# Degree inverses of a graph network: made per block inside a pipeline, or for all blocks ahead of it

## What is computed

```
x = layernorm(x + segment_sum(w * x[src], dst) @ W0.T)        # layer 0
x = layernorm(x + L1(x))   # two GCN convolutions with batch norm, then a dense layer
x = layernorm(x + L2(x))   # weighted sum over edges, two-layer MLP
x = layernorm(x + L3(x))   # one GCN convolution with layer norm
# a GCN convolution:
deg  = segment_sum(1, dst) + 1        # with self loops
dinv = 1 / sqrt(deg)
out[d] = sum over edges of (x @ W)[s] * dinv[s] * dinv[d]
```

## Time and profile before

| | before |
|---|---|
| time, median of 3 runs | 3458.49 us |
| profiled execution: time | 3460.09 us |
| profiled execution: span of its trace | 3458.8 us |
| outside the span | 1.3 us |
| block pipeline: first load issued, last load issued | 1270.4, 1375.2 us |

### The profile page before, as it was taken

How to read it: one execution, slowest core, us unless ns; L and a number is a source line. 1 busy time by engine, 2 the same in 40 slices (tenths; PEclk the granted TensorE clock), 3 DMA queues, 4 the chain that set the end, 5 groups by cost and what they waited for, 6 DMA issues and landing times. The chain is left out here.

```text
span 3458.8 us, 60258 instructions
## 1 busy us (share of the span) xinstructions
PE 2842.7 (82%) x19203; PEld 2100.9 (61%) x19220; DVE 1983.2 (57%) x6763; ACT 1275.6 (37%) x3485; POOL 2462.4 (71%) x2238
## 2 busy tenths in 40 slices
PE   5989877878888859789977997778888875699995
PEld 4777655656666648444446774366666764466664
DVE  7889777777787729442243434443444564245557
ACT  5566666776877739200010002500111232001123
POOL 3888777786676667577747776777777774777773
PEclk8999998999999979899978997589999998799996
DMA  8787788888888879678856886755556564988884
GB/s 273 112 147 113 142 154 148 155 155 170 179 175 170 180 175 354 180 213 231 237 141 177 226 224 172 217 172 158 162 176 181 159 178 124 297 235 247 252 251 137
DMA packets 658436, 652.79 MB, mean 189 GB/s; under 512 B 87902, under 2 KB 606476, under 8 KB 656588
## 3 DMA queue, kind: packets, MB, share of 16 engines
q0 software_dynamic: 153600, 258.41, 37.3%
q1 hardware_dynamic: 430670, 331.83, 31.2%
q10 hardware_dynamic: 73854, 58.70, 5.4%
HBM read 434.19 MB, written 214.52 MB: 188 GB/s over the span
## 5 line engine op out<-in xcount | busy, mean ns | idle before, releaser
L1701 POOL DMA_INDIRECT A<-rows_buf,big x572 | 902.4, 1578 | 333.8 <-issue 143.5
L882 POOL DMA_INDIRECT rows_buf<-T,idx x888 | 847.7, 955 | 275.9 <-issue 272.2
L976 PE MATMUL PSA<-S,rows_buf 128*128 128x128 bf16 (+2 forms) x5904 | 582.5, 254 | 213.9 <-DMA rows_buf<-X,idx 103.5
L976 PEld LDWEIGHTS PSA<-S,rows_buf 128*128 128x128 bf16 (+2 forms) x5904 | 523.3, 142 | 296.8 <-DMA rows_buf<-X,idx 88.0
L882 POOL DMA_INDIRECT rows_buf<-X,idx x528 | 509.5, 965 | 160.9 <-issue 157.8
L1032 DVE TENSOR_TENSOR accT<-PSA,accT 128x256 f32 (+2 forms) x354 | 132.8, 375 | 835.7 <-PE PSA L976 828.5
L1556 DVE TENSOR_TENSOR accT<-PSA,accT 128x392 f32 (+5 forms) x366 | 239.7, 655 | 173.0 <-issue 59.6
L1394 PE MATMUL PSA<-XRS,rows_buf 128*128 128x256 f32 x1144 | 313.0, 398 | 6.4 <-ACT rows_buf L1406 6.4
L793 ACT ACTIVATE accT<-accT,vec 128x500 f32<-128x500 f32 (+3 forms) x26 | 17.7, 693 | 666.5 <-DVE accT L791 666.4
L1406 ACT ACTIVATE rows_buf<-PSA 128x512 f32<-128x512 f32 x286 | 168.0, 593 | 186.1 <-PE PSA L1394 175.8
L1394 PEld LDWEIGHTS PSA<-XRS,rows_buf 128*128 128x128 f32 x1144 | 209.8, 197 | 32.0 <-ACT rows_buf L1385 6.8
(11 more groups left out here) (315 smaller groups left out, 5805.3 us busy)
## 6 DMA issues: line engine op xcount, KB each, us to landing
XRS<-Ad SPq DMA_DIRECT2D x400, 256.0 KB
Ad<-accT SPq DMA_DIRECT2D x224, 196.0 KB
XRS<-in_xpad SPq DMA_DIRECT2D x192, 128.0 KB, 3.3
Awd<-accT SPq DMA_DIRECT2D x48, 392.0 KB, 3.6
A<-accT SPq DMA_DIRECT2D x9, 1600.0 KB
rows_buf<-T,idx POOLq DMA_INDIRECT x888
rows_buf<-A SPq DMA_DIRECT2D x24, 512.0 KB
accT<-A SPq DMA_DIRECT2D x24, 512.0 KB, 6.1
```

Of the source, the lines that this page charges most:

```text
L882: s_hg[slot(i)][j // 2].on(pool.indirect_dma_start(Gv(slot(i), j), None, table, bass.IndirectOffsetOnAxis(idx[:, c:c + 1], 0)), 16)
L976: last = pe.matmul(PS[bank_of(i)][0:F, W * h:W * h + W], Gv(slot(i), j)[:, o:o + F], hits[:, i % SRING, j, :], start=j + part == 0, stop=j ...
L1701: s_k[n].on(pool.indirect_dma_start(A, bass.IndirectOffsetOnAxis(tgt[:, c:c + 1], 0), G[:, i % RING, j, :], None, compute_op=ALU.add), 16)
```

## The change

The matmul that stands up the degrees, the square root and the reciprocal leave the pipeline. A new `degree_inverses()` runs ahead of it: 49 matmuls into 49 columns of PSUM bank 7, two square roots (48 full columns, and the last of 106 rows) and two reciprocals. `turn_sums` keeps its two transposes and now counts `s_ta` on the second of them. `spread_degrees` and `degrees_out` stay; the wait for the reciprocal is made once, at t = 0.

```diff
         for h in range(2):
-            pe.transpose(PS[t % 2][:, 128 * h:128 * h + r], part_sums[slot][0:r, 0, 128 * h:128 * h + 128], ident[0:r, 0:r])
-        s_ta.mark(t, pe.matmul(PS[t % 2][0:r, 256:257], degB[0:1, cols(t)], ones[0:1, 0:1], start=True, stop=True))
+            ins = pe.transpose(PS[t % 2][:, 128 * h:128 * h + r], part_sums[slot][0:r, 0, 128 * h:128 * h + 128], ident[0:r, 0:r])
+        s_ta.mark(t, ins)
@@ sums_out
-        s_nq.mark(t, sc.activation(dnm[0:rows(t), t:t + 1], PS[t % 2][0:rows(t), 256:257], ACT.Sqrt))
         s_ca.mark(t, sc.activation(sumT[:, t % 4, :, 0:rows(t)], p, ACT.Identity))
-    def degree_inverses(t):
-        s_nq.of(v, t)
-        s_dr.mark(t, v.reciprocal(dnm[0:rows(t), t:t + 1], dnm[0:rows(t), t:t + 1]))
+    def degree_inverses():
+
+        for t in range(NT):
+            ins = pe.matmul(PS[7][0:rows(t), t:t + 1], degB[0:1, cols(t)], ones[0:1, 0:1], start=True, stop=True)
+        s_dq.on(ins)
+        s_dq.by(sc)
+        r = rows(NT - 1)
+        sc.activation(dnm[:, 0:NT - 1], PS[7][:, 0:NT - 1], ACT.Sqrt)
+        s_nq.on(sc.activation(dnm[0:r, NT - 1:NT], PS[7][0:r, NT - 1:NT], ACT.Sqrt))
+        s_nq.by(v)
+        v.reciprocal(dnm[:, 0:NT - 1], dnm[:, 0:NT - 1])
+        s_dr.on(v.reciprocal(dnm[0:r, NT - 1:NT], dnm[0:r, NT - 1:NT]))
     def spread_degrees(t):
-        s_dr.of(pe, t)
+        if t == 0:
+            s_dr.by(pe)
         s_ca.of(pe, min(t + 1, NT - 1))
@@ the pipeline
-    pipeline([(0, load_sums), (2, add_pairs), (3, add_last), (4, turn_sums), (5, sums_out), (6, degree_inverses), (7, spread_degrees), (8, degrees_out), (4, residual(a["xpad"])),
+    degree_inverses()
+    pipeline([(0, load_sums), (2, add_pairs), (3, add_last), (4, turn_sums), (5, sums_out), (7, spread_degrees), (8, degrees_out), (4, residual(a["xpad"])),
-             + table_rows(16, ..., lambda t: (s_tc.of(pe, t), s_dr.of(sc, t)), queue=sc))
+             + table_rows(16, ..., lambda t: (s_tc.of(pe, t), s_dr.by(sc)), queue=sc))
```

More of the change, by code:

```diff
@@ L2067, in build @@
              + [(14, store(ZR0, X1)), (14, transpose(lambda t: zs(ZR0, t), s_nm)), (15, turned(xT))]
-             + table_rows(16, T1, 128, lambda i, t: xT[:, i, cols(t)], [W1[:, 0, :], W1[:, 1, :]], lambda t: (s_tc.of(pe, t), s_dr.of(sc, t)), queue=sc))
+             + table_rows(16, T1, 128, lambda i, t: xT[:, i, cols(t)], [W1[:, 0, :], W1[:, 1, :]], lambda t: (s_tc.of(pe, t), s_dr.by(sc)), queue=sc))
     s_do.by(v)
```

## The result

The changed kernel takes 3471.18 us (median of 6 runs, 3467.76 to 3475.19), the kernel before, measured beside it, 3457.55 us. The ratio is 1.0037, with a 95% interval from 1.0026 to 1.0048: slower by 13.6 us, and by more than 0.2%. The forecast was 3471.5 us, 12.9 us above the kernel before. The profiled execution of after took 3468.2 us (span 3467.0).

What follows compares the result with a forecast made beforehand. PE was taken to bound the kernel at 2.36 us per block, the DMAs 2% behind at about 2.32. Terms 15.8 - 1.4 - 1.0 - 0.5 = +12.9 us gave 3471.5 us on the median's scale, range 3459 to 3480.

Steps and rivals of the forecast that it cites:

- stream of 98 passes: Ahead of the pipeline on PE: 49 float32 matmuls at clock 0.50 take 21.2 us, bounds 14.2 and 28.4.
- `add_last(0)` later by: DVE's first addition waits for all 49 matmuls, table load, roots and reciprocals: 17.5 us later.
- load 8 later by: SP issues this load only after block 0 is through PE and DVE: 15.8 us later, DMAs idle meanwhile.
- loads 8 to 16: After the delayed load 8, empty DMA queues win back some time: -1.0 us, bounds -3 and +2.
- loads 16 to 48: Full pipeline: with less PE work the DMAs limit at about 2.32 us per block, -1.4 us over 75 us.
- landing of load 48: Last load, from issue to use: 14 us that no engine can shorten, so no change.
- from there to the end of the stage: Behind the last load, block 48 loses two PE passes and a bit of ACT: -0.5 us.
- The rival with a rising clock: PE's clock rises during the new matmuls, which end about 5 us earlier: +8 us, 3466.5 us; chance 0.08.
- The queue: Head of the pipeline: `add_last(0)` waits behind DVE's wait, load 8 behind `residual(4)`; load 8 comes 15.8 us later.
- The relief: Full pipeline: PE loses 0.31 to 0.48 us per block, but the DMAs allow only 0.04: -1.4 us.
- rival 1: Full pipeline: the DMAs have room and PE alone bounds, giving 3453.6 to 3460.4 us; chance 0.12.
- The small terms: Refill behind load 8, -1.0 us; last load's landing, fixed at 14 us; work behind it, -0.5 us.

Runs made afterwards that it cites:

- e2_both: Kernel before with the 49 matmuls, two roots and two reciprocals added ahead of the pipeline, per-block work kept; 16.1 us above the kernel before.
- e3_onepass: Changed kernel with its 49 two-pass float32 matmuls replaced by 49 one-pass transposes; median 6.6 us under the kernel before, ratio interval 0.9977 to 1.0002.
- e4_wide: Changed kernel with each of the 49 matmuls moving 128 columns instead of one; 11.5 us above the kernel before, ratio interval 1.0015 to 1.0035.
- e7_chain: Changed kernel with ACT's table loaded earlier and the reciprocals moved behind step 6 of the pipeline; 6.7 us above the kernel before.
- p9_before: Kernel before with two of four partial sums loaded and POOL's addition cut to a one-element copy; 2.4 us below the kernel before.
- e1_none: Changed kernel without any degree work, dnm set to one; 3.1 us below the kernel before, ratio interval 0.9983 to 1.0001.
- e8_dma: Changed kernel with the 49 matmuls replaced by one DMA and one transpose, one root and one reciprocal; 1.2 us below the kernel before.

## Why the prediction was right, and where it wasn't

Each step in us, forecast and measured (after less before, from the first profiles):

| step | forecast | measured |
|---|---|---|
| stream of 98 passes | 21.2 | 20.96 |
| `add_last(0)` later by | 17.5 | 17.2 |
| load 8 later by | 15.8 | 15.2 |
| loads 8 to 16 | -1.0 | -3.2 |
| loads 16 to 48 | -1.4 | -1.1 |
| landing of load 48 | 0 | +1.4 |
| from there to the end of the stage | -0.5 | +0.7 |
| sum | +12.9 | +13.1 |

The sum is made of unrounded terms. (On the scale of the median the forecast's own sum gives 3471.4 us, not 3471.5.)

**The stream.** Right to 0.3 us, because the kernel already had a row of 98 float32 passes back to back at low clock. The rival with a rising clock fell: 0.50 from its first pass to its last. The Trainium skill, TensorE: Matmul & The Clock Gate, Part 1, has the throttle released by activity; a PE that is busy without a gap for 21 us, with one column a pass or with 128, was not granted the full clock here. It was granted from 1291.5 us on, behind the first product of 256 columns, as PE's timeline of after shows:

```profile
1287.82 1.11 PE L1982 MATMUL PSA<-ident,rows_buf 128*128 128x128 f32 x4 [2.62 <-DVE rows_buf L1974]
1288.98 2.07 PE L641 MATMUL PSA<-weights,accT 128*128 128x256 f32 x4
...
1291.49 1.03 PE L641 MATMUL PSA<-weights,accT 128*128 128x256 f32 x4
...
1292.68 1.03 PE L641 MATMUL PSA<-weights,accT 128*128 128x256 f32 x4
```

The first product takes 2.07 us, the second 1.03.

**The queue.** DVE's wait in front of `add_last(0)`, and SP's `residual(4)` in front of load 8, did what was forecast: `residual(4)` is issued right at the end of `add_residual(0)`, load 8 behind it, and until then the DMA share is 0.08 for 14 us. The run with a shorter chain made load 8 2.7 us earlier and the stage 1.8 to 2.0 us shorter, and the run with 49 single passes took the head away.

**The relief.** The size was right (0 to 1 us, shown by the runs with the head alone and the relief alone), and the period was right: 885 kB per block at the 378 GB/s that after moves between 1310 and 1360 us is 2.34 us, and the spacing of its transposes is 2.32 us, as forecast. That the loads set it shows in the waits of after in this stretch. These two rows are of the slots called rows_buf; with those called accT, POOL waits for 22 loads and DVE for 22 of POOL's sums:

```profile
POOL rows_buf L1969 <- DMA rows_buf<-A: 9.2, 12, 1.8
DVE rows_buf L1974 <- POOL rows_buf L1969: 9.0, 12, 1.7
```

PE could go to 1.86 us, just below the 1.88 to 2.05 us of the forecast. But the reason was too narrow. I wrote that neither ACT nor DVE ends a wait of PE, "so both count nothing", and that the DMAs are what is late next. In the changed kernel the DMAs are full indeed (share 1.09). But with half the loads the period doesn't fall. Below PE's 2.36 us stand the DMAs at 2.32 and ACT at about 2.1, and DVE, held up by POOL, comes to 2.47 when the loads no longer set the pace. (With full loads it has 14 us of gaps in 50, and `add_last` takes 0.63 us.) And "count nothing" held in the kernel before only: in the changed one PE's gaps end on ACT's copy 15 times of 19. That the row of rival 1 gave 3453.6 to 3460.4 us for "the DMAs have room" was wrong for the same reason: with room on the DMAs the difference stayed at 13.1 us.

**The small terms.** The refill behind load 8 won back 2.2 us more than I took, just past its bound of -3. I had counted on a low clock for the loads 9 to 11; but the clock was up before load 8, and load 9 follows it after 1.46 us, where it took 3.05 in the kernel before. In the second pair of profiles the term is -1.9 us, so it scatters by 1.3. The landing of the last load, which I took as fixed at 14.05 us, took 15.5 and 15.2 us in both profiles of the changed kernel. But with full loads it takes 13.7 us in e2_both, which has the same head, and 15.7 in e3_onepass, which has almost none; so the change is not shown to lengthen it. A stretch within it shows few DMA engines at work:

```profile
1387.40:1388.40 1.00, 1.00 (x7) 0.83 (x7) 1.00 (x6) 1.00 (x5) 0.00 (x0) 1.00 0.13 47
```

A share of 0.13 of 16 engines is two of them, at 47 GB/s. The Trainium skill, DMA: Bandwidth & Descriptors, section "Why a DMA increments its semaphore by 16 and not by 1", spreads a transfer over the largest number of engines, up to 16, that divides its rows; for the 106 rows of the last block that is 2. The trace agrees. Why the landing takes 13.7 us in one run and 15.7 in another stays open. The last stretch grew by 0.2 to 0.7 us (two pairs of profiles) instead of shrinking by 0.5. These errors cancelled: the sum is closer than its terms deserve.

## What to carry to other kernels

Work that is taken out of a pipeline and put ahead of it is hidden only for as long as its engine would have waited anyway (here 6.4 us of 21), and what it delays are the loads that are queued behind the first results, not only the engine that does it. Before counting a relief, list every limit down to the period that the relieved engine could reach (here 1.86 us): there were three ahead of that, and taking one away showed only the next. And look for the cheaper form of a small operation: a transpose did in one pass of 0.109 us what the float32 matmul did in two of 0.214.

## What the runs showed of the hardware

- With a weight of one row, a float32 matmul with one moved column costs as much as with 128: 98 passes took 20.96 and 21.24 us at 1.2 GHz. Between these two the number of moved columns does not set the price. The single pass of a transpose of one row costs 0.109 us at the same clock.
- PE was granted 0.50 for some 21 us of unbroken passes in four kernels (the changed one, e2_both, e4_wide, e7_chain).
- DVE's addition of two SBUF tensors of 128x256 takes 0.41 us with POOL's additions taken away (p9_before), and 1.0 us in the median of the kernel before, where it overlaps them. The addition of the same size that has one input in PSUM (line 2014; line 2023 in the changed kernel) takes 0.40 to 0.43 us, beside POOL's additions too. The Trainium skill, SBUF — State Buffer, section "SBUF: two separate sides", has DVE and GpSimd (POOL) share a pair of ports that one of them holds for a whole instruction, a DVE instruction with two SBUF inputs against a GpSimd one that reads SBUF among them; that agrees with DVE's rows ending 0.28 us after POOL's.
- On two of the chips the kernel before took 3835 us instead of 3451 to 3458, while the block stage is no longer there as far as the edited kernels tell (145.6 to 146.7 us in e1_none and e8_dma).
